# A graph layer with routed experts on one core: a 28-slot result ring laid over the gather ring, a gather loop of 28 groups, and five smaller edits

## The reference

```python
xn = layernorm(x)
m = (xn @ gnn_w + gnn_b)[src]                      # one row per edge
gnn = segment_sum(m, dst, 6250) / maximum(degree, 1)
q, k, v = elu1(xn@wq+bq), elu1(xn@wk+bk), xn@wv+bv # linear attention, 8 heads
mix = ((q @ sum(k^T v)) / (q @ sum(k) + 1e-6)) @ wo + bo
x1 = x + gnn + mix
xn1 = layernorm(x1)
expert = argmax(softmax(xn1 @ gate_w + gate_b))    # 8 experts, top 1
# a token keeps its place if it is among the first C = 977 of its expert
y = (relu(xn1 @ w1[e] + b1[e]) @ w2[e] + b2[e]) * prob * kept
out = x1 + nan_to_num(y)
```

## Time and profile before

| | us |
|---|---|
| median of 3 runs (lowest, highest) | 1432.51 (1428.54, 1433.97) |
| the profiled execution, its span | 1431.63, 1429.7 |
| PE busy, share of the span | 1118.5, 78% |
| POOL busy | 920.5, 64% |
| DVE busy | 828.1, 58% |
| ACT busy | 554.1, 39% |

### The profile page before, as it was taken

The page is one execution under the profiler, slowest core; times in us unless marked ns, Lnnn a source line. Parts: engine busy times, 40 slices in busy tenths (PEclk is TensorE's granted clock), DMA queues, the critical chain, the costliest instruction groups (busy, mean ns, idle before and its releaser), DMA issues.

```text
span 1429.7 us, 33109 instructions
## 1 busy us (share of the span) xinstructions
PE 1118.5 (78%) x5801; PEld 788.8 (55%) x5802; DVE 828.1 (58%) x2795; ACT 554.1 (39%) x1433; POOL 920.5 (64%) x967
## 2 busy tenths in 40 slices
PE   3769876857767877888768778787888888888996
PEld 2456543534444445666545555565655665666885
DVE  6754432746757666667545555565666666666343
ACT  4822221322323223434334334443454454455342
POOL 4746776777777776767667676666766657622741
PEclk9579996979979889999989999999999999999998
DMA  7593334444545455645455555555554655644762
GB/s 221 193 294 104 104 104 128 121 137 125 148 138 157 145 152 166 191 136 170 151 167 148 165 177 170 159 177 164 180 175 156 204 166 171 203 143 136 237 213 89
DMA packets 143365, 231.72 MB, mean 162 GB/s; under 512 B 29824, under 2 KB 87329, under 8 KB 143248
## 3 DMA queue, kind: packets, MB, share of 16 engines
q0 software_dynamic: 42896, 115.65, 27.2%
q1 hardware_dynamic: 99118, 114.27, 25.6%
q10 hardware_dynamic: 1234, 0.66, 0.2%
HBM read 197.40 MB, written 35.08 MB: 163 GB/s over the span
## 4 chain that ended last, share of the span: by engine, by line
issue 25%; PE 22%; POOL 22%; DVE 13%; DMA 6%; ACT 3%; DVEq 3%; POOLq 3%; SPq 1%; ACTq 0%; PEldq 0%
POOL shared L597 18%; PE pA L928 6%; PE pH L1058 4%; DMA shared<-table,idx 4%; PE pY L1049 3%; POOL out_dram L544 3%; DVE shared L1429 3%; PE pQ L972 2%; PE pT L980 2%; DMA shared<-in_L_ffn_w_dram 1%; PE pD L986 1%; DVEq L1377 1%; PE pX L1026 1%; DVE shared L1435 1%; PE pH L908 1%
## 5 line engine op out<-in xcount | busy, mean ns | idle before, releaser
L597 POOL DMA_INDIRECT shared<-table,idx x784 | 767.2, 979 | 329.7 <-issue 286.2
L928 PE MATMUL pA<-shared,onehot 128*128 x976 | 284.3, 403 | 144.1 <-POOLq L577 81.2
L928 PEld LDWEIGHTS pA<-shared,onehot 128*128 x976 | 92.2, 99 | 321.8 <-issue 245.8
L1369 DVE TENSOR_TENSOR onehot<-tile_iota,dst_t 128x512 f32 x244 | 160.4, 695 | 104.3 <-PE pA L928 66.1
L1049 PE MATMUL pY<-w2s,shared 128*128 x864 | 207.3, 394 | 13.5 <-issue 9.3
L1058 PE MATMUL pH<-shared 128*128 128x128 f32 x1728 | 202.8, 275 | 5.5 <-DMA shared<-in_L_ffn_w_dram 5.4
L1058 PEld LDWEIGHTS pH<-shared 128*128 128x128 f32 x1728 | 201.3, 192 | 10.0 <-DMA shared<-in_L_ffn_w_dram 7.4
L1049 PEld LDWEIGHTS pY<-w2s,shared 128*128 128x128 f32 x864 | 164.9, 196 | 39.8 <-issue 18.0
L779 ACT ACTIVATE shared<-pH,b1s 128x128 f32<-128x128 f32 x432 | 122.1, 372 | 78.5 <-PE pH L1058 68.3
L714 ACT ACTIVATE shared<-pA 128x256 f32<-128x256 f32 (+1 forms) x49 | 20.7, 423 | 251.9 <-PE pA L928 251.9
L1411 DVE TENSOR_SCALAR tile_iota<-tile_iota 128x128 f32<-128x128 f32 x48 | 12.9, 269 | 181.6 <-PE pA L928 162.5
(11 more groups left out here) (251 smaller groups left out, 1644.1 us busy)
## 6 DMA issues: line engine op xcount, KB each, us to landing
shared<-in_L_ffn_w_dram SPq DMA_DIRECT2D x108, 512.0 KB
shared<-table,idx POOLq DMA_INDIRECT x784
w2s<-in_L_ffn_w_dram SPq DMA_DIRECT2D x8, 1024.0 KB, 7.0
rows<-rows_sb SPq DMA_DIRECT2D x7, 1040.0 KB, 14.7
shared<-rows SPq DMA_DIRECT2D x54, 130.0 KB
shared<-in_L_ffn_b_dram SPq DMA_DIRECT2D x54, 128.0 KB
shared<-in_x_dram SPq DMA_DIRECT2D x12, 512.0 KB, 8.3
table<-w2s SPq DMA_DIRECT2D x12, 512.0 KB, 3.8
```

Of the source, the lines that this page charges most:

```text
L597: g.indirect_dma_start(gathered[:, s * G + j, :], None, table[:, :], bass.IndirectOffsetOnAxis(ap=idx[:, q * G + j:q * G + j + 1], axis=0) ...
L928: m = pe.matmul(pA[:, :], onehot[:, n % OQ, j, :], gathered[:, (f % RQ) * G + j, :], start=False, stop=final and j == G - 1)
L1369: v.tensor_tensor(onehot[:, n % OQ, :, :], tile_iota[:, :].rearrange("p (a n) -> p a n", a=1).broadcast_to([P, G, P]), dst_t[:, bass.ds(ch ...
```

## The change

1. `fin` becomes 28 slots (FB = RING) and lies over the memory of the gather ring; `post` waits once more, for the last scatter, before it writes there. The tree of `finish` has 28 leaves.
2. TRIPS goes from 2 to 4: the body has 28 groups, the loop runs Fori(1, 7) instead of Fori(1, 14). The index buffer keeps its size.
3. `load_end` reads the tile's end from `ends`, where DVE already puts it, instead of working it out from the packed word; `ends` is widened to 64 columns and filled with a large number.
4. SP's step loads weights ahead of rows; in the tail, bias ahead of weights.
5. 8 of the 44 kept results are sent ahead of the last events, 6 more ahead of the very last event.
6. In PE's `add` the two slot addresses are kept in registers that are stepped and wrapped; the group numbers are shifted by one, so that waits need no addition, and one semaphore instruction is gone.
7. `plan` and the count of the tail use min(count, SLOTS), SLOTS = 1024, where they had CAP = 977. (Rows beyond the 977th are still not scattered; their places hold rows that are not sent.)

```diff
-TRIPS = 2
+TRIPS = 4
-IDX = BODY * G
-HALF = IDX // 2
+HALF = RQ * G
+IDX = 2 * HALF
+SENT = (8, 14)
-FB = 4
+FB = RING
+got_of = [shared[:, 0:RING * D].bitcast(F16)[:, j * 2 * D:(RING - G + j + 1) * 2 * D] for j in range(G)]
-fin = part_of(FB * D).rearrange("p (a d) -> p a d", a=FB)
+fin = shared[:, 0:FB * D].rearrange("p (a d) -> p a d", a=FB)
+one_of = [onehot...[:, j * P:(OQ * G - G + j + 1) * P] for j in range(G)]
 # SP, step
+                if weights:
+                    load_weights(t - T0 + 1, weights == "first")
                 if rows:
                     load_rows(t - T0 + 2, t * 16 - 16, rows == "first")
-                if weights:
-                    load_weights(t - T0 + 1, weights == "first")
 # SP, tail
                 load_rows(i + (J0 + 2), 16 * NT + 16)
+                load_bias(i + J0)
                 load_weights(i + (J0 + 1))
-                load_bias(i + J0)
 # POOL
-                g.load(reg, words[0:1, bass.ds(t, 1)])
-                w = g.snap(reg)
-                g.reg_mov(reg, w // PACK + w % PACK)
-                g.reg_add(reg, reg, -1)
+                g.load(reg, ends[0:1, 2, bass.ds(t, 1)])
-                with g.While(lambda: g.snap(tend) < f - LAG):
+                with g.While(lambda: g.snap(tend) < f - LAG + 1):
...
-                with g.Fori(g.snap(tile), NT) as t:
+                for j in range(SENT[0]):
+                    send_kept(j)
+                with g.Fori(g.snap(tile), NT - 1) as t:
                     event(t)
-            for j in range(KEPT):
+            for j in range(SENT[0], SENT[1]):
+                send_kept(j)
+            event(NT - 1)
+            for j in range(SENT[1], KEPT):
                 send_kept(j)
 # PE, add
-                    n = pe.snap(pair_r)
-                    pe.wait_ge(S["relayed"], f + 1)
-                    pe.sem_inc(S["pe_hold"], 1)
-                    pe.wait_ge(S["oh_ready"], n + 1)
+                    pe.wait_ge(S["relayed"], f)
+                    pe.reg_add(got_r, got_r, G * 2 * D)
+                    pe.reg_alu(got_r, got_r, RING * 2 * D, ALU.python_mod)
+                    pe.wait_ge(S["oh_ready"], pair_r)
+                    pe.reg_add(one_r, one_r, G * P)
+                    pe.reg_alu(one_r, one_r, OQ * G * P, ALU.python_mod)
+                    got = pe.snap(got_r, min_val=0, max_val=(RING - G) * 2 * D)
+                    one = pe.snap(one_r, min_val=0, max_val=(OQ - 1) * G * P)
                     for j in range(G):
-                        m = pe.matmul(pA[:, :], onehot[:, n % OQ, j, :], gathered[:, (f % RQ) * G + j, :], start=False,
+                        m = pe.matmul(pA[:, :], one_of[j][:, bass.ds(one, P)], got_of[j][:, bass.ds(got, 2 * D)], start=False,
...
 # DVE, plan and the count of the tail
-k(v.scalar_tensor_tensor(pend[0:1, 0, :], pX[...], float(CAP), first_row[0:1, :], ALU.min, ALU.add))
+k(v.scalar_tensor_tensor(pend[0:1, 0, :], pX[...], float(SLOTS), first_row[0:1, :], ALU.min, ALU.add))
 # DVE, post
                     if r is not None:
+                        v.wait_ge(S["scat_done"], 16 * NT + 16)
+                        v.sem_inc(S["dve_hold"], 1)
                         v.wait_ge(S["fin_free"], j + 1)
```

More of the change, by code:

```diff
@@ L200, in gps_block @@
         planw = sb("planw", [1, PB], I32)
-        ends = sb("ends", [1, 3, NT], I32)
+        ends = sb("ends", [1, 3, 64], I32)
         idx = sb("idx", [P, IDX], I32)
         onehot = sb("onehot", [P, OQ, G, P], F16)
+        one_of = [onehot[:, :, :, :].rearrange("p a b c -> p (a b c)")[:, j * P:(OQ * G - G + j + 1) * P] for j in range(G)]
         sel_f = onehot[:, :, :, :].rearrange("p a b c -> p (a b c)").bitcast(F32)
@@ L577, in report, with copy_idx @@
                 g.sem_inc(S["relayed"], 1)
[L579 to L582 removed]
+            def copy_idx(i, trip):
+                o = trip % 2 * HALF
+                g.tensor_copy(idx[:, o:o + HALF], src_t[:, bass.ds((i % TURNS) * (BODY * G) + trip * HALF, HALF)]).then_inc(S["idx_ok"], 1)
             def gather(i, q, tile=None, tend=None):
@@ L597, in gather @@
                     g.indirect_dma_start(gathered[:, s * G + j, :], None, table[:, :],
-                                         bass.IndirectOffsetOnAxis(ap=idx[:, q * G + j:q * G + j + 1], axis=0)).then_inc(landed[s], 16)
+                                         bass.IndirectOffsetOnAxis(ap=idx[:, q * G % IDX + j:q * G % IDX + j + 1], axis=0)).then_inc(landed[s], 16)
                 if not (first and q == 0):
@@ L601, in gather @@
                 if q % RQ == 0:
-                    copy_idx(i if q == 0 else i + 1, 1 if q == 0 else 0)
+                    last = q // RQ == TRIPS - 1
+                    copy_idx(i + 1 if last else i, 0 if last else q // RQ + 1)
             g.wait_ge(S["e_copied"], 2)
@@ L913, in _ @@
             pe.sem_inc(S["oh_slots"], OQ - 1)
-            with pe.register("held") as at_r, pe.register("pair") as pair_r, pe.register("now") as now_r, pe.register("last") as last_r:
-                pe.reg_mov(at_r, 0)
-                pe.reg_mov(pair_r, 1)
+            with pe.register("held") as at_r, pe.register("pair") as pair_r, pe.register("now") as now_r, pe.register("last") as last_r, \
+                 pe.register("one") as one_r, pe.register("got") as got_r:
+                pe.reg_mov(at_r, 1)
+                pe.reg_mov(pair_r, 2)
+                pe.reg_mov(one_r, 0)
                 def load_span(t):
@@ L938, in sum_start @@
                     lo = pe.snap(w // PACK)
-                    pe.reg_mov(now_r, lo)
-                    pe.reg_mov(last_r, lo + w % PACK - 1)
+                    pe.reg_mov(now_r, lo + 1)
+                    pe.reg_mov(last_r, lo + w % PACK)
+                    pe.reg_mov(got_r, (lo + (RQ - 1)) % RQ * (G * 2 * D))
                     at_ = pe.snap(at_r)
-                    with pe.If(at_ < lo):
-                        with pe.Fori(at_, lo) as f:
-                            pe.wait_ge(S["relayed"], f + 1)
+                    with pe.If(at_ < lo + 1):
+                        with pe.Fori(at_, lo + 1) as f:
+                            pe.wait_ge(S["relayed"], f)
                             pe.sem_inc(S["slots"], 1)
@@ L1546, in plan @@
                     k = part("plan_c", j)
-                    k(v.scalar_tensor_tensor(pend[0:1, 0, :], pX[0:1, GW + NX:GW + 2 * NX], float(CAP), first_row[0:1, :], ALU.min, ALU.add))
+                    k(v.scalar_tensor_tensor(pend[0:1, 0, :], pX[0:1, GW + NX:GW + 2 * NX], float(SLOTS), first_row[0:1, :], ALU.min, ALU.add))
                     k(v.scalar_tensor_tensor(pend[0:1, 0, :], next_tile_[0:1, :], float(-P), pend[0:1, 0, :], ALU.mult, ALU.add))
@@ L1659, in _ @@
                 v.wait_ge(S["plan_c"], PLANNED * K["plan_c"])
-                c(v.scalar_tensor_tensor(lg[0:1, 0, :], pX[0:1, GW + NX:GW + 2 * NX], float(CAP), first_row[0:1, :], ALU.min, ALU.add))
+                c(v.scalar_tensor_tensor(lg[0:1, 0, :], pX[0:1, GW + NX:GW + 2 * NX], float(SLOTS), first_row[0:1, :], ALU.min, ALU.add))
                 c(v.scalar_tensor_tensor(lg[0:1, 0, :], next_tile_[0:1, :], float(-P), lg[0:1, 0, :], ALU.mult, ALU.add))
```

13 lines of the change are left out of this document (7 added, 6 removed).

## The result

The changed kernel takes 1368.57 us (median of 4 runs, 1366.48 to 1369.73) against 1430.53 for the kernel before on the same chip (4 runs, 1424.48 to 1433.97): a ratio of 0.957, 95% interval 0.9532 to 0.9607. It was forecast at 1384, inside 1362 to 1412. The profiled execution took 1369.36 us.

What follows compares the result with a forecast made beforehand. POOL's gather bounds up to about 400 and 687 to 911 us, DVE 911 to 1290, PE the tail. Terms -17.1 - 2.7 - 8 - 16.2 - 4.4 + 0.5 = -47.9 from 1431.6, plus 0.9: 1384, range 1362 to 1412.

Steps and rivals of the forecast that it cites:

- DVE is no floor: Rival: DVE's steps after 911 us shrink; last stretch gives 24 us, gather 26, ending at 1362; chance 0.08.
- DVE as the floor behind tile 24: From 911 to 1290 us DVE sets the pace; at most 10 us to gain, 8 taken.
- The planner's count: Tail: counting to 1024 instead of 977 gives 52 jobs, not 54; -16.2 us, bounds 15 to 18.
- The register edit: PE's add saves 0.2 us a group, but POOL and DVE cover it, so no term of its own.
- the 0.5 us of the sum for the tree: Tail: the deeper branch tree adds some 0.5 us to the last result.
- the loop's jumps: POOL's gather up to 911 us: jumps back that vanish with the longer body save 17.1 us, bounds 0 to about 26.
- weights ahead of rows: After 911 us: PE's 6.5 us of waits for weights go, as part of the 10 us there.
- bias in the tail, -4.4: Tail: ACT's 45.9 us of waits for bias hold up PE; up to 5.4 us to gain, 4.4 taken.
- eight and six results sent early, 0: POOL's last events: sending kept results ahead of them changes nothing, taken as 0, bounds -3 to +3 us.
- the tile's end, -2.7: 687 to 911 us: loading the end without division or remainder saves 2.7 us over eleven events, 0 if covered.
- Rows too late: Rival: rows come 2.1 us later behind the weights and 43 steps lose 90 us, giving 1474; chance 0.06.
- The tree is fetched anew: Rival: in the tail the 28-leaf tree's code is fetched for every result, some 37 us late, 1421; chance 0.06.

Runs made afterwards that it cites:

- e8: Changed kernel with CAP (977) again in the planner and the tail's count, instead of SLOTS: 1381.53 us, ratio 0.9668 to the kernel before.
- e5: Changed kernel with PE's add as before (slot numbers divided in the operands, one semaphore instruction more): 1370.91 us, ratio 0.9598 to the kernel before.
- e10: Changed kernel with a result ring of 4 slots instead of 28: 1369.75 us, ratio 0.9588 to the kernel before.
- e3: Changed kernel with a 14-group body again and 80 idle increments that keep the first gather's code place: 1374.35 us, ratio 0.9628 to the kernel before.
- e2: Kernel before with 64 idle semaphore increments added ahead of the first gather, moving the loop's code: 1411.76 us, ratio 0.9888.
- e12: Kernel before with only weights moved ahead of rows in SP's step: 1408.32 us, ratio 0.9872.
- e7: Changed kernel with rows put back ahead of weights in SP's step: 1383.71 us, ratio 0.9684 to the kernel before.
- e9: Changed kernel with the second bias put back behind the weights in SP's tail: 1366.57 us, ratio 0.9583 to the kernel before.
- e11: Changed kernel with all 44 kept results sent behind the last event: 1373.31 us, ratio 0.9632 to the kernel before.
- e6: Changed kernel with the tile's end worked out by division and remainder again: 1368.25 us, ratio 0.9578 to the kernel before.
- e4: Changed kernel with TRIPS = 14, a body of 98 groups and no jump back: 1358.94 us, ratio 0.9531 to the kernel before.

## Why the prediction was right or wrong

**Right in mechanism.** The range held in part by luck: its lower end was set by the rival "DVE is no floor", and by the bounds of its own terms the sum would have ended at 1372. DVE as the floor behind tile 24 held: 15.35 us a step, -10.8 measured for -8. The planner's count held to the job: 52 jobs, 8 results, with -14.8 in the profile (e8), just below the lower bound of 15, where -16.2 was taken: two jobs more cost 7.4 each, not the mean of 8.1; the runs have 13 to 14. The register edit needed no term (e5). Neither ring nor tree cost anything (e10), and the ring gave nothing; the 0.5 us of the sum for the tree has no row behind it.

**Mis-sized: the loop's jumps.** The step took the gaps of the five jumps that vanish up to 911, 17.1 us, as gained in full, with no gain on the jumps that stay. The runs split it: at a kept place five jumps are worth 8.5 us at tile 24 (e3), and the place of the code, which no edit meant to change, is worth 13.2 there and 17 at the end (e2). In a row: before to e2 -13.2, e2 to e3 (all other edits) -11.6, e3 to the changed kernel -8.5 make the -33.2 at tile 24, each good to some 6 us; the order of the loads alone (e12, -11.9) is as large as the middle step. The step also read the gap at 808.77 as 1.70, though an event stood ahead of that gather and the whole gap behind the jump was 4.3 without the event's own DMA; and it missed that the jumps ahead of groups 56, 84, 112 and 140 could get cheaper. These four got 9.8 us cheaper.

**Wrong: weights ahead of rows.** The step took this as 6.5 us of PE's waits behind tile 24, "part of the 10 us", and nothing ahead of it. It is worth 15 us undone (e7) and 19 alone (e12), of which 11.9 are there at tile 24. What failed was to price a reordered queue by the waits of the one engine that uses its data. SP waited 33.8 us for events while the weights stood behind the rows, and gathers issued just behind such weights landed late and held POOL, by 9.2 us in the kernel before and 1.1 in e12.

**Wrong: bias in the tail, -4.4.** 45.9 us of ACT's waits were read as holding up PE. e9 shows that they are exchanged for another wait.

**Wrong: eight and six results sent early, 0.** POOL would end the kernel without them (e11), 5 us. The forecast asked what a late event costs and not when POOL's 44 sends would be through. This error and the bias's nearly cancel, so the tail's sum looked right.

**Wrong: the tile's end, -2.7.** Nothing (e6).

**The rivals.** "DVE is no floor" had nearly the measured time, 1362, by the wrong cause: its 24 us behind tile 24 were 10.8, and its 26 to tile 24 were 33. "Rows too late" happened at 18 steps and cost nothing, since DVE's step is longer. "The tree is fetched anew" fell with e10. Of the signs named ahead, jobs, results and branch count came as said; the gaps behind the jumps that stay did not stay as large as before.

**What single edits add up to.** Undone singly, the order (15.1 by medians), CAP (13.0), the body (5.8), the early sends (4.7), `add` (2.3) and the place (2.6) give 43.5 of 62 us. By the ratios the same six give 57, so the runs do not decide whether something is left over. The place alone was worth 17 in the kernel before and 2.6, or 5.6 by the ratios, in the changed one; part of that is that nine jumps stood ahead of tile 24 and four do now. That the edits share one slack of POOL against PE is possible and not shown.

## What to carry to other kernels

A gap behind a loop's jump is not one price: look whether the queue stalls once or twice, and move the code by a few dozen idle instructions before paying for unrolling; here that alone gave 1.1%. When a transfer is moved in a queue, look at what the queue waits for ahead of it and at whose transfers it then leaves beside, not only at the waits of the engine that reads the data. A wait on an engine off the path is worth nothing until it is shown that no other wait takes its place.

## What the runs showed of the hardware

The queue of POOL, right behind a jump back, stopped twice when the loop's first gather stood one past a multiple of 256 by the count above: 4.1 and 3.1 us at group 112 of the kernel before. With 64 idle instructions ahead of it the gap fell from 5.11 to 0.81 us, and the whole kernel from 1429.2 to 1411.76 us on the same chip. Straight code of 98 groups (e4) has 0.30 us at groups 56 and 112; its 2.44 us at group 84 are a report that waits for a landing, not a fetch. In the kernel before, gathers issued within 2.9 us behind a half of weights (512 KB) landed up to 7.2 us behind their issue, where the mean of groups 98 to 139 is 3.75.
